# Attention beside a routed feed-forward layer on one core: heads normalised and stacked in pairs before the output projection, and another order of work where attention begins

## The chip, the core and the metric

The kernel runs on one core of a Trainium2 chip. The metric is the device time of one execution in microseconds (us). Five engines work side by side, each through its own list in order, and wait for each other by semaphores: TensorE (PE in the profile), VectorE (DVE), ScalarE (ACT), GpSimd (POOL) and SyncE (SP), which here only issues DMAs.

## The reference

Four sequences of 1024 tokens of 128 features are layer-normalised. The result goes through causal attention with 16 heads of 64 features, and through a mixture of 8 experts (two per token), whose sum is layer-normalised again. Both are added to the input.

```python
x = L0_attn_x
xn = _layernorm(x, axis=-1)
x = x + _L0_attn_ref(xn, ...) + _L0_ffn_ref(xn, ...)

# attention
normed = xn / l2 * dim ** 0.5 * gamma
q, k, v = split(normed @ w_qkv)          # 16 heads of 64
sim = einsum('bhid,bhjd->bhij', q * d ** (-0.5), k)
attn = softmax(where(causal_mask, mask_value, sim))
out = einsum('bhij,bhjd->bhid', attn, v)
return merge_heads(out) @ w_out          # 1024 -> 128
```

## The kernel before

The first block (up to about 284 us) normalises the tokens, chooses two experts for each, writes the tokens sorted by expert to DRAM, and runs the experts tile by tile; the results go back to DRAM by DMAs from ACT's queue. Then a barrier of all engines, and the second block: attention, and beside it the gathering and combining of the experts' results.

Attention goes over 8 pairs of heads (`hp`), in each over the 4 sequences, in each over the two heads of the pair: 64 rounds, which the text calls heads, 0 to 63. An even head and the odd one behind it are one pair on one sequence. A head's 1024 x 1024 score matrix, transposed (keys on partitions), is worked through in 12 chunks, c = 0 to 11: half 0 of the queries has chunks 0 to 3, half 1 chunks 4 to 11, each of 128 keys by 128 to 512 queries. `beside(g, c, last)` writes down what stands at chunk c of head g, and every engine walks the same list:

- `score` (lines 1302 to 1320): two matmuls, and a third one of the mask on the diagonal. ACT takes the exponential twice, once as float32 (`probs`), once rounded (`p_hi`), line 1082; POOL subtracts the two (`p_lo`, line 1033).
- `pv` (L1333, L1335, L1337), four chunks behind: three matmuls with the values; row 64 of the result, from a column of ones, is the softmax's denominator. After the last chunk of a half ACT copies the 65 x 512 result to `heads` (L1096).
- `max` (L1291, L1294 on PE, L1135 on DVE): the row maxima of the next head, in 8 parts, of which 4 to 7 are wide (640 to 1024 keys). They share one PSUM tile, so that PE's part m waits for DVE's part m-1 or m-2. `shift` turns the maxima by a transpose (L1300), ACT negates them, and SP lays them as a row of `q_b` by a DMA (L966); the first score of a half waits for it.
- `project` (L1261 to L1267): q, k and v of the next pair, with ACT's rounded copies (L1057, L1061), DVE's remainders (L1125, L1113), and four copies of 256 KB by SP (L954, L955).
- `y` and `add`, at chunks 6, 9 and 10: the output projection of the head before. A token tile is one matmul of 65 x 128 weights (the head's numerators and denominator) with the 65 x 129 matrix `wo`, whose corner passes the denominator on (L1350). DVE inverts it (L1191) and adds the scaled tile to `acc` (L1199).
- `combine` and `gather`: the experts' results, in heads 1 to 5 of each group of 8.

float32 matmuls count twice in the trace (two passes): `y` of a head has 8 matmuls, 16 passes, in groups of 6, 6 and 4.

The second block begins with splitting the first projection weights into a rounded part (ACT, L1048) and a remainder (DVE, L1105); then six projections, eight maxima and the first `shift` of head 0, and then the chunks.

## Time and profile before

| | |
|---|---|
| median of 3 runs | 1565.51 us (1565.09 to 1565.91) |
| the profiled execution | 1564.66 us |
| its span, first to last instruction | 1562.8 us |
| mean granted clock of TensorE | 0.969 |
| PE busy | 1449.6 us (93%) |
| DVE busy | 1076.4 us (69%) |
| ACT busy | 1067.4 us (68%) |
| POOL busy | 907.1 us (58%) |

A row of a timeline is: start in us, duration in us, engine, line and operation, output<-inputs with their forms, how many follow each other in it; in brackets the idle time before it and what ended that. PEld is the weight load of a matmul. Matmuls overlap, and a matmul's duration is longer than the distance to the next one: what a group of them costs PE is read from start to start.

### The profile page before, as it was taken

The numbers are of one execution on the slowest core, as the hardware profiler recorded it, in microseconds if no ns is written. First come the engines' busy times: TensorE is split into PE (matmuls) and PEld (weight loads), VectorE is DVE, ScalarE is ACT, GpSimd is POOL, SyncE is SP. The second block draws the span as 40 slices with busy tenths as digits, with TensorE's granted clock in tenths as the row PEclk, the third lists the DMA queues.
The fourth block names the chain that finished last, engine by engine and source line by source line (L and its number), as shares of the span: only waits on it lengthen the run. The fifth ranks groups of instructions, "written<-read, shape, count | busy, mean of one in ns | idle before, by whom it ended". The sixth has DMA issues, their size and how long they took to land.

```text
span 1562.8 us, 28739 instructions
## 1 busy us (share of the span) xinstructions
PE 1449.6 (93%) x9130; PEld 1126.8 (72%) x9131; DVE 1076.4 (69%) x2341; ACT 1067.4 (68%) x2590; POOL 907.1 (58%) x923
## 2 busy tenths in 40 slices
PE   3559999699999999999999999999999999999998
PEld 3548888467777777777777777777777777777776
DVE  6565555457776877687768776876687668866883
ACT  2445566267777777777777777777777777777775
POOL 0762000157666766676667666766676667666766
PEclk9579999689999999999999999999999999999999
DMA  9122211111111111111111111111111111111111
GB/s 311 46 79 71 58 54 52 44 35 42 33 28 38 40 33 29 38 40 33 29 38 40 33 28 40 38 33 28 39 38 33 28 41 37 33 28 42 37 28 55
DMA packets 58759, 72.34 MB, mean 46 GB/s; under 512 B 7400, under 2 KB 44560, under 8 KB 58640
## 3 DMA queue, kind: packets, MB, share of 16 engines
q1 hardware_dynamic: 40720, 52.57, 14.2%
q10 hardware_dynamic: 13824, 9.86, 2.0%
q0 software_dynamic: 4096, 8.40, 1.8%
q8 instruction: 65, 1.06, 0.3%
q14 instruction: 54, 0.44, 0.1%
HBM read 20.47 MB, written 16.52 MB: 24 GB/s over the span
## 4 chain that ended last, share of the span: by engine, by line
PE 66%; DVE 9%; ACT 3%; issue 2%; DMA 1%; SPq 0%; POOLq 0%; POOL 0%; DVEq 0%; ACTq 0%
PE max_ps L1291 9%; PE score_ps L1316 8%; PE score_ps L1317 8%; PE misc_ps L1350 8%; PE head_ps L1333 7%; PE head_ps L1337 7%; PE head_ps L1335 7%; PE misc_ps L1267 3%; DVE q_a L1125 3%; PE max_ps L1294 2%; PE score_ps L1319 2%; DVE row_max L1135 2%; ACT p_hi L1082 1%; PE misc_ps L1261 1%; PE misc_ps L1300 1%
## 5 line engine op out<-in xcount | busy, mean ns | idle before, releaser
L1033 POOL TENSOR_TENSOR p_lo<-probs,p_hi 128x512 fp32r<-128x512 f32 (+3 forms) x768 | 775.0, 1025 | 415.1 <-ACT p_hi L1082 408.7
L1082 ACT ACTIVATE probs<-score_ps 128x512 f32<-128x512 f32 (+3 forms) x768 | 375.4, 489 | 236.2 <-PE score_ps L1319 168.6
L1135 DVE TENSOR_REDUCE row_max<-max_ps 128x1 f32<-128x128 f32 (+7 forms) x512 | 386.7, 756 | 157.2 <-PE max_ps L1294 146.7
L1082 ACT ACTIVATE p_hi<-score_ps 128x512 fp32r<-128x512 f32 (+3 forms) x768 | 373.2, 486 | 0.0
L1333 PE MATMUL head_ps<-p_hi,v_hi 128*65 128x512 f32 (+3 forms) x768 | 295.2, 384 | 0.3 <-POOL p_lo L1033 0.3
L1316 PE MATMUL score_ps<-q_a,k_a 128*128 128x512 f32 (+3 forms) x768 | 266.6, 347 | 3.1 <-DMA q_b<-shift 3.1
L1317 PE MATMUL score_ps<-q_b,k_b 65*128 65x512 f32 (+3 forms) x768 | 266.9, 348 | 0.0
L1291 PE MATMUL max_ps<-k_a,q_a 128*128 128x384 f32 (+5 forms) x768 | 249.6, 380 | 16.4 <-DVE row_max L1135 12.6
L1337 PE MATMUL head_ps<-p_lo,v_hi 128*65 128x512 f32 (+3 forms) x768 | 258.7, 337 | 0.0
L1335 PE MATMUL head_ps<-p_hi,v_lo 128*64 128x512 f32 (+3 forms) x768 | 258.5, 337 | 0.0
L1316 PEld LDWEIGHTS score_ps<-q_a,k_a 128*128 128x128 f32 x768 | 144.8, 189 | 46.4 <-issue 3.7
L1291 PEld LDWEIGHTS max_ps<-k_a,q_a 128*128 128x128 f32 x768 | 144.6, 197 | 40.0 <-DVE row_max L1135 19.5
L1317 PEld LDWEIGHTS score_ps<-q_b,k_b 65*128 65x128 f32 x768 | 145.4, 189 | 16.7
L1350 PE MATMUL misc_ps<-wo,heads 65*128 65x129 f32 x1024 | 155.9, 285 | 1.3 <-ACT heads L1096 0.8
L1199 DVE SCALAR_TENSOR_TENSOR acc<-misc_ps,rden,acc 128x128 f32<-128x128 f32 x512 | 150.1, 345 | 6.8
L1337 PEld LDWEIGHTS head_ps<-p_lo,v_hi 128*65 128x65 f32 x768 | 104.0, 135 | 42.0
L1350 PEld LDWEIGHTS misc_ps<-wo,heads 65*128 65x128 f32 x1024 | 131.5, 194 | 2.0 <-issue 1.2
L1294 PE MATMUL max_ps<-ident,later 128*128 128x128 bf16 x512 | 118.8, 232 | 0.0
L1319 PE MATMUL score_ps<-later,ident 128*128 128x128 bf16 x512 | 118.7, 232 | 0.0
L1125 DVE TENSOR_TENSOR k_b<-misc_ps,k_a 64x512 fp32r<-64x512 f32 x128 | 88.1, 688 | 43.1 <-ACT k_a L1057 42.2
L1335 PEld LDWEIGHTS head_ps<-p_hi,v_lo 128*64 128x64 f32 x768 | 105.4, 137 | 15.2
L1333 PEld LDWEIGHTS head_ps<-p_hi,v_hi 128*65 128x65 f32 x768 | 108.7, 141 | 8.5 <-POOL p_lo L1033 0.8
(170 smaller groups left out, 2106.0 us busy)
## 6 DMA issues: line engine op xcount, KB each, us to landing
k_a<-k_a SPq DMA_DIRECT2D x64, 256.0 KB, 3.3
q_b<-q_a SPq DMA_DIRECT2D x64, 256.0 KB, 4.2
sorted_x<-zeros SPq DMA_DIRECT2D x13, 384.0 KB, 15.2
w_raw<-sorted_x SPq DMA_DIRECT2D x26, 192.0 KB, 2.5
sorted_y<-result ACTq DMA_DIRECT2D x78, 64.0 KB, 1.6
acc<-in_L_attn_x_dram SPq DMA_DIRECT2D x4, 512.0 KB, 9.0
w_raw<-in_L_ffn_W_dram ACTq DMA_DIRECT2D x1, 2048.0 KB, 22.7
q_b<-shift SPq DMA_DIRECT2D x128, 2.0 KB
```

What stands on the lines that cost most here:

```text
L1033: pool.tensor_tensor(p_lo[:, slot, 0:w], probs[:, slot, 0:w], p_hi[:, slot, 0:w].bitcast(F32), ALU.subtract).then_inc(p_split, 1)
L1082: ins = act.activation(p[:, (g * CH + c) % RING, 0:width], score_ps[(g * CH + c) % 2][:, 0:width], ACT.Exp, scale=SCALE)
L1135: dve.tensor_reduce(row_max[:, g % 2, t:t + 1], src, axes, ALU.max).then_inc(max_taken, 1)
L1199: ins = dve.scalar_tensor_tensor(out=row, in0=src[:, t, 0:D], scalar=rden[:, u % 2, t:t + 1], in1=row, op0=ALU.mult, op1=ALU.add)
L1291: ins = pe.matmul(max_ps[:, b, 0:w], rows, k_a[i][s][:, k0:k0 + w], start=True, stop=not last)
L1294: ins = pe.matmul(max_ps[:, b, w - P:w], later[:], ident16[:], start=False, stop=True)
L1316: pe.matmul(dst, k_a[i][s][:, keys], q_a[i][s][:, qs], start=True, stop=False)
L1317: ins = pe.matmul(dst, k_b[i][s][:, keys], q_b[i][s][:, qs], start=False, stop=not DIAG[c])
L1333: pe.matmul(head_ps[0:HEAD + 1, cols], v_hi[i][:, j, s], p_hi[:, slot, 0:width], start=(j == 0), stop=False)
L1335: pe.matmul(head_ps[0:HEAD, cols], v_lo[i][:, j, s], p_hi[:, slot, 0:width], start=False, stop=False)
L1337: pe.matmul(head_ps[0:HEAD + 1, cols], v_hi[i][:, j, s], p_lo[:, slot, 0:width], start=False, stop=c in LAST).then_inc(pv_done, 1)
L1350: ins = pe.matmul(dst[:, t * (D + 1):(t + 1) * (D + 1)], heads[:, g % 2, q0:q0 + P], wo[:, g % 2], start=True, stop=True)
```

## The change

1. **Stacked heads.** ACT's copy of a half (65 x 512) goes to `raw`. From there a chain of five steps runs in the list, at fixed numbers of chunks behind the last chunk of the half: SP folds the denominator row by a DMA to 16 x 32 (`fold`, 5), DVE inverts it (`invert`, 8), SP stores it to DRAM (`store`, 9), SP reads it back to 64 partitions (`spread`, 12), DVE multiplies the 64 x 512 numerators by it (`normalise`, 16) into `heads`, the even head of a pair in partitions 0 to 63, the odd one in 64 to 127. The output projection then has 128 rows and 128 columns without the denominator, once for the pair: four tiles (8 passes) at chunk 8 of the next even head, four at chunk 4 of the odd one behind it. DVE adds 128 x 512 in one instruction.
2. **Straight code.** The list is made once for all 64 heads; its counters are plain. `probs` has 4 buffers instead of 6, with a wait of ACT for POOL.
3. **Weights among the set-up work.** The split of the first projection weights stands in the first block. The wait for the experts' stored results goes from ACT's end of the first block to SP and POOL, ahead of the first gather.
4. **Wide maxima of the first head.** Only parts 0 to 3 stand ahead of its chunks; 4 and 5 stand at chunk 0, 6 at chunk 1, 7 at chunk 2. Head 1's maxima begin at chunk 3.

```diff
@@ set-up
+                    w_hi(act, 0)
                     act.wait_ge(set_up, 7)
                     act.sem_inc(waited, 1)
                     expert_steps(act, step)
-                    for n in range(RESULTS):
-                        act.wait_ge(expert_stored[n], 16 * (1 + len(range(n, SORTED, RESULTS))))
...
                         lower(u)
+                    w_lo(dve, 0)
...
@@ the list
+            CHAIN = [("fold", 5), ("invert", 8), ("store", 9), ("spread", 12), ("normalise", 16)]
+            FIRST_WIDE = {0: (4, 5), 1: (6,), 2: (7,)}
+            FIRST_MAX_AT = [3, 4, 5, 6, 7, 8, 9, 10]
-            Y_AT = [6, 9, 10]
-            y_units = [(0, 3), (3, 3), (6, 2)]
+            Y_AT = {8: 0, CH + 4: 1}
...
+                for kind, lag in CHAIN:
+                    if at >= lag and (at - lag) // CH < ALL_HEADS and (at - lag) % CH in LAST:
+                        order.append((kind, (at - lag) // CH, LAST.index((at - lag) % CH)))
...
@@ SP
+                    def fold_denominator(g, half):
+                        sp.wait_ge(raw_out, n_half(g, half) + 1)
+                        sp.dma_start(den[:, half], raw[HEAD:HEAD + 1, g % 2, half].rearrange("o (f n) -> o f n", f=FOLD)
+                                     ).then_inc(den_folded[half], 16)
+                    def store_inverse(g, half):
+                        sp.wait_ge(inverted, n_half(g, half) + 1)
+                        sp.dma_start(inv_rows[half].rearrange("(f n) -> f n", f=FOLD), inv[:, half]
+                                     ).then_inc(inv_stored[half], 16)
+                    def spread_inverse(g, half):
+                        sp.wait_ge(inv_stored[half], 16 * g + 16)
+                        sp.dma_start(scale[:, half], inv_rows[half].partition_broadcast(HEAD)
+                                     ).then_inc(scale_spread[half], 16)
...
@@ ACT
+                            if n_chunk(g, c) >= PROBS:
+                                act.wait_ge(p_split, n_chunk(g, c) - PROBS + 1)
...
+                            if g >= 2:
+                                act.wait_ge(normalised, n_half(g - 2, half) + 1)
+                            act.activation(raw[:, g % 2, half], head_ps[0:HEAD + 1, cols],
+                                           ACT.Copy).then_inc(raw_out, 1)
...
@@ DVE
+                    def invert(g, half):
+                        dve.wait_ge(den_folded[half], 16 * g + 16)
+                        dve.reciprocal(inv[:, half], den[:, half]).then_inc(inverted, 1)
+                    def normalise(g, half):
+                        cols = slice(half * BANK, (half + 1) * BANK)
+                        s = g % 2
+                        dve.wait_ge(scale_spread[half], 16 * g + 16)
+                        dve.tensor_tensor(heads[s * HEAD:(s + 1) * HEAD, cols], raw[0:HEAD, s, half], scale[:, half],
+                                          ALU.mult).then_inc(normalised, 1)
+                    def add_y(p, n, u):
...
+                        dve.wait_ge(misc_ready, u + 1)
+                        dve.tensor_tensor(acc[:, toks], misc_ps[u % 2][:].rearrange("p (t d) -> p t d", t=GROUP),
+                                          acc[:, toks], ALU.add).then_inc(y_added, 1)
...
@@ PE
+                    def project_out(p, n, u):
+                        dst = misc_bank(u)
+                        pe.wait_ge(normalised, n_half(2 * p + 1, n) + 1)
...
+                        for t in range(GROUP):
+                            q0 = (n * GROUP + t) * P
+                            ins = pe.matmul(dst[:, t * D:(t + 1) * D], heads[:, q0:q0 + P], wo[:],
+                                            start=True, stop=True)
+                        ins.then_inc(misc_ready, 1)
```

DVE in head 16 (an even one), chunks 5 to 10: `k_b` are the key remainders, `row_max` the maxima of head 17, `rden` and `acc` the inversion and addition of the output projection. Before:

```order
L1125 TENSOR_TENSOR k_b10<-misc_ps0,k_a10 64x512
L1125 TENSOR_TENSOR k_b11<-misc_ps0,k_a11 64x512
L1135 TENSOR_REDUCE row_max<-max_ps 128x1
L1191 RECIPROCAL rden<-misc_ps1 128x3
L1199 SCALAR_TENSOR_TENSOR acc<-misc_ps1,rden,acc 128x128 x3
L1135 TENSOR_REDUCE row_max<-max_ps 128x1
L1191 RECIPROCAL rden<-misc_ps1 128x3
L1199 SCALAR_TENSOR_TENSOR acc<-misc_ps1,rden,acc 128x128 x3
L1135 TENSOR_REDUCE row_max<-max_ps 128x1
```

The same place of the changed kernel:

```order
L1129 TENSOR_TENSOR k_b10<-misc_ps1,k_a10 64x512
L1129 TENSOR_TENSOR k_b11<-misc_ps1,k_a11 64x512
L1139 TENSOR_REDUCE row_max<-max_ps 128x1
L1193 RECIPROCAL inv<-den 16x32
L1199 TENSOR_TENSOR heads<-raw,scale 64x512
L1139 TENSOR_REDUCE row_max<-max_ps 128x1
L1206 TENSOR_TENSOR acc<-misc_ps1,acc 128x512
L1139 TENSOR_REDUCE row_max<-max_ps 128x1
```

Between the maxima of parts 5 and 6 the inversion and the multiplication of two earlier halves stand where the additions of the head before stood.

PE in head 16, chunks 6 to 9: `max_ps` are the maxima of head 17, `head_ps` the values, `misc_ps<-wo,heads` the output projection. Before:

```order
L1317 MATMUL score_ps0<-q_b00,k_b00 128x512
L1291 MATMUL max_ps<-k_a01,q_a01 128x448 x2
L1294 MATMUL max_ps<-ident16,later 128x128
L1350 MATMUL misc_ps1<-wo,heads 128x129 x3
L1333 MATMUL head_ps<-p_hi,v_hi0 65x384
...
L1291 MATMUL max_ps<-k_a01,q_a01 128x384 x2
L1294 MATMUL max_ps<-ident16,later 128x128
L1333 MATMUL head_ps<-p_hi,v_hi0 65x512
```

The same place of the changed kernel:

```order
L1316 MATMUL score_ps0<-q_b00,k_b00 128x512
L1290 MATMUL max_ps<-k_a01,q_a01 128x448 x2
L1293 MATMUL max_ps<-ident16,later 128x128
L1332 MATMUL head_ps<-p_hi,v_hi0 65x384
...
L1290 MATMUL max_ps<-k_a01,q_a01 128x384 x2
L1293 MATMUL max_ps<-ident16,later 128x128
L1346 MATMUL misc_ps1<-wo,heads 128x128 x4
L1332 MATMUL head_ps<-p_hi,v_hi0 65x512
```

The output projection leaves chunk 6 and stands at chunk 8, behind the part of the maxima that waits for DVE.

PE at the first head, from its fourth maximum on. Before:

```order
L1291 MATMUL max_ps<-k_a00,q_a00 128x512
L1294 MATMUL max_ps<-ident16,later 128x128
L1291 MATMUL max_ps<-k_a00,q_a00 128x512 x2
L1294 MATMUL max_ps<-ident16,later 128x128
...
L1291 MATMUL max_ps<-k_a00,q_a00 128x320 x2
L1294 MATMUL max_ps<-ident16,later 128x128
L1300 MATMUL misc_ps0<-ident,row_max 4x128
L1316 MATMUL score_ps0<-q_a00,k_a00 128x512
```

The same place of the changed kernel:

```order
L1290 MATMUL max_ps<-k_a00,q_a00 128x512
L1293 MATMUL max_ps<-ident16,later 128x128
L1299 MATMUL misc_ps0<-ident,row_max 4x128
L1315 MATMUL score_ps0<-q_a00,k_a00 128x512
L1316 MATMUL score_ps0<-q_b00,k_b00 128x512
L1318 MATMUL score_ps0<-later,ident16 128x128
L1290 MATMUL max_ps<-k_a00,q_a00 128x512 x2
L1293 MATMUL max_ps<-ident16,later 128x128
L1290 MATMUL max_ps<-k_a00,q_a00 128x448 x2
L1293 MATMUL max_ps<-ident16,later 128x128
```

The four wide maxima, ahead of the first score before, stand behind it.

## Rows read from the trace of the kernel before

**Rows 1.** Busy time by engine in a steady stretch: us, busy us (instructions) of each, clock, DMA

```profile
500.00:1000.00 500.00, 490.36 (x3098) 372.81 (x3098) 367.78 (x757) 371.33 (x855) 343.51 (x342) 1.00 0.16 36
```

**Rows 2.** Chain of waits, longest pieces: start us, us, what; once in eight heads

```profile
531.38 1.19 DVE gsc L1144
...
686.75 1.19 DVE gsc L1144
```

**Rows 3.** Timeline of head 16, an even one, chunks 6 to 9

```profile
639.49 0.89 PE L1350 MATMUL misc_ps<-wo,heads 65*128 65x129 f32 x6
...
640.13 0.42 PE L1333 MATMUL head_ps<-p_hi,v_hi 128*65 128x384 f32 x1
...
640.56 1.09 DVE L1135 TENSOR_REDUCE row_max<-max_ps 128x1 f32<-128x896 f32 x1
...
640.92 1.98 POOL L1033 TENSOR_TENSOR p_lo<-probs,p_hi 128x512 fp32r<-128x512 f32 x2 [1.20 <-ACT p_hi L1082]
...
641.98 0.52 PE L1291 MATMUL max_ps<-k_a,q_a 128*128 128x384 f32 x2
...
642.38 0.42 PE L1333 MATMUL head_ps<-p_hi,v_hi 128*65 128x512 f32 x1
```

**Rows 4.** Timeline of head 17, an odd one, chunks 3 to 5

```profile
652.49 1.84 POOL L1033 TENSOR_TENSOR p_lo<-probs,p_hi 128x384 fp32r<-128x384 f32 x2 [1.10 <-ACT p_hi L1082]
...
653.22 0.69 DVE L1135 TENSOR_REDUCE row_max<-max_ps 128x1 f32<-128x512 f32 x1 [0.82 <-PE max_ps L1294]
...
654.70 0.43 PE L1333 MATMUL head_ps<-p_hi,v_hi 128*65 128x512 f32 x1
...
655.66 1.11 PE L1267 MATMUL misc_ps<-w_raw,nT 128*128 128x128 f32 x8
...
656.53 0.30 PE L1333 MATMUL head_ps<-p_hi,v_hi 128*65 128x128 f32 x1
```

**Rows 5.** Groups by line and form: count, busy us, mean ns, idle before

```profile
L1181 DVE TENSOR_TENSOR x_row<-x_row,fbeta 128x512 f32<-128x512 f32 x8 | 5.4, 681 | 0.0
L1184 DVE TENSOR_TENSOR acc<-acc,x_row 128x512 f32<-128x512 f32 x8 | 13.4, 1669 | 0.3
L477 DVE RECIPROCAL tmp<-tmp 128x16 f32<-128x16 f32 x2 | 0.5, 253 | 0.1
L1350 PE MATMUL misc_ps<-wo,heads 65*128 65x129 f32 x1024 | 155.9, 285 | 1.3 <-ACT heads L1096 0.8 <-DVE acc L1199 0.5
```

**Rows 6.** Timeline of DVE in head 11, where the experts' results are combined

```profile
543.35 0.87 DVE L1199 SCALAR_TENSOR_TENSOR acc<-misc_ps,rden,acc 128x128 f32<-128x128 f32 x3
...
546.57 0.94 DVE L1135 TENSOR_REDUCE row_max<-max_ps 128x1 f32<-128x768 f32 x1
```

**Rows 7.** Timeline of the passage to attention

```profile
282.44 2.02 ACTq L425 DMA_DIRECT2D sorted_y<-result  x2
...
287.33 0.79 PE L1261 MATMUL misc_ps<-nT_hi,wqk_hi 128*128 128x512 f32 x1 [3.76 <-DVE wqk_lo L1105]
...
304.11 1.39 DVE L1135 TENSOR_REDUCE row_max<-max_ps 128x1 f32<-128x384 f32 x2 [0.32 <-PE max_ps L1294]
...
313.67 0.42 PE L1300 MATMUL misc_ps<-ident,row_max 128*4 128x128 f32 x1
...
314.42 9.38 SPq L966 DMA_DIRECT2D q_b<-shift  x2
...
316.28 0.76 PE L1316 MATMUL score_ps<-q_a,k_a 128*128 128x512 f32 x1 [2.19 <-DMA q_b<-shift]
```

**Rows 8.** Timeline of the last head's end

```profile
1554.66 0.59 ACT L1096 ACTIVATE heads<-head_ps 65x512 f32<-65x512 f32 x1 [2.37 <-PE head_ps L1337]
...
1558.52 0.61 DVE L1199 SCALAR_TENSOR_TENSOR acc<-misc_ps,rden,acc 128x128 f32<-128x128 f32 x2
```

**Rows 9.** DMA issues: what, queue, count, KB each, median us from issue to landing

```profile
sorted_y<-result ACTq DMA_DIRECT2D x78, 64.0 KB, 1.6
...
fgamma<-in_L_ffn_gamma_dram SPq DMA_DIRECT2D x1, 64.0 KB, 2.8
```

More of the change, by code:

```diff
@@ new lines, in attention_and_experts, with n_max, n_chunk, n_half @@
+            order += [("max", 0, m) for m in range(HALF_MAX[0] + 1)] + [("shift", 0, 0)]
+            for at in range(ALL_HEADS * CH + 2 * CH):
+                order += beside(at)
+            order = numbered(order)
+            misc_units = [o[:3] for o in order if o[0] in MISC_KINDS]
+            def n_max(g, m):
+                return g * PARTS + m
+            def n_chunk(g, c):
+                return g * CH + c
+            def n_half(g, half):
+                return g * 2 + half
+            def n_y(p, n):
+                return p * 2 + n
@@ new lines, in _ @@
+                    for kind, g, c, u in order:
+                        if kind == "score":
+                            score(g, c)
+                        elif kind == "max":
+                            max_scores_of(g, c)
+                        elif kind == "project":
+                            project(g, c, u)
+                        elif kind == "shift":
+                            shifts(g, c, u)
+                        elif kind == "pv":
+                            values(g, c)
+                        elif kind == "y":
+                            project_out(g, c, u)
```

448 lines of the change are left out of this document (188 added, 260 removed).

## The prediction, written before the changed kernel ran

> **What bounds the kernel now.** I read the busy times by window first. In a steady stretch of 500 us PE is busy 490.4 us at full clock, DVE 367.8, ACT 371.3 and POOL 343.5 [rows 1]. So the end is set by what stands in PE's list and by PE's few waits. The chain of waits shows a period: the same piece of the combination comes at 531.38 and at 686.75, so eight heads take 155.37 us [rows 2], 19.42 us a head. The reader should see that an engine with a quarter of its time free can still be late at one place, and PE has almost no free time in which that would be hidden. So I went from the shares to the timeline of an even and an odd head, at the places where the output projection leaves and arrives.
>
> **Passes of the output projection.** A group of 6 passes takes PE from 639.49 to 640.13, 0.64 us, or 0.107 a pass [rows 3]. A head has 16 passes, 1.71 us. Eight passes of 128 x 128 with 128 rows, which is what the new form has, take from 655.66 to 656.53, 0.87 us [rows 4]. The changed kernel has 8 passes a head on average, so a head loses 0.84 us of PE's list, 64 heads 53.8 us. The busy time of the group is 155.9 us for 1024 passes [rows 5], 0.152 a pass, but matmuls overlap there; the Trainium skill (Perfetto Trace Analysis, Identifying the Most-Contended Engine) says that matmul busy time is a bad measure because PE's instructions are pipelined. The spacing bears this out, and I take the spacing.
>
> **What PE now waits for, even head.** The projection left chunk 6 and stands at chunk 8, behind part 6 of the maxima. Before, it filled a hole: part 6 may start only when DVE has reduced part 5, at 640.56 + 1.09 = 641.65, and PE came there at 641.98 [rows 3]. DVE's reduction does not come earlier, since its input stands ahead of the projection in PE's list, and DVE went straight on to it from the key remainders. With the 0.64 us gone PE arrives at 641.34 and waits 0.31. Part 6 takes 0.40 (641.98 to 642.38), so PE is ready for the new projection at 642.05. That waits for `normalise`, which stands on DVE behind part 5 and the inversion. The inversion is 16 x 32; a 16-element reciprocal takes 0.253 [rows 5], twice that would be 0.51, and I take 0.38: until 642.03. The multiplication is not in the trace before. The nearest row is a float32 multiplication or addition of 128 x 512 with both inputs in SBUF: 0.681 us, but the like at another place takes 1.669 [rows 5]. What differs is whether POOL, which reads SBUF, is in an instruction. POOL is in two of them from 640.92 to 642.90 [rows 3]; by their widths (512 and 256) the first ends near 642.24. So the multiplication runs from 642.24 to 642.92, and the projection waits 0.87. Together 1.18 us of waiting in an even head, against 0.84 of passes saved: +0.34 us.
>
> The Trainium skill (SBUF — State Buffer, Who interferes with whom) says that a DVE instruction with two SBUF inputs contends with a GpSimd instruction that reads SBUF, and that the one issued second is fully blocked until the first is finished. The 1.669 beside the 0.681 agrees with it. The additions that go (L1199) have one input in PSUM, so this rule speaks against the change: the multiplications are 128 new instructions that can be blocked.
>
> **Odd head.** `normalise` stands behind part 3, which ends at 653.22 + 0.69 = 653.91; POOL is in two instructions from 652.49 to 654.33 [rows 4]. So it ends at 654.33 + 0.68 = 655.01. PE is at the projection's place at 654.70, where its next row starts now, and waits 0.31. With -0.84 this is -0.53 us.
>
> **Head 11 and its like**, one in eight, has DVE full of the combination. Part 6 is reduced at 546.57 [rows 6]. Ahead of it come new: two multiplications (1.36), the addition of 128 x 512 (0.68, by the same row), the inversion (0.38) and about 0.3 for the port; one addition of 0.87 goes [rows 6]. So part 6 is 1.85 later, and PE's part 7 with it. The four passes at chunk 10 (0.43) give some back: +1.4 us. In head 13, DVE's other full place, an inversion comes and a small addition goes; nothing.
>
> Eight heads: 4 x 0.34 - 3 x 0.53 + 1.4 = +1.2 us; eight times, +9.4. Heads 0 and 1 have no projection yet, which takes 0.3 + 1.2 = 1.5 off.
>
> **Edits that I cost at nothing.** ACT's wait for POOL with four buffers of `probs`: POOL is busy 343.5 of 500 us and PE itself needs the same result at the end of the chunk in which ACT needs it at the start. It would cost up to PE's whole loss of the wait, some 0.3 us a chunk, if POOL fell a chunk behind. The three DMAs of the chain: from SP's issue of the shift at 314.42 to the score that waited for it, 316.28, is 1.86 us [rows 7]; three times this and the inversion are 6 us, and the chain has 12 chunks of 1.6 us. Behind the chain's DMAs on SP stands the next shift, which needs to be there three chunks later; issue costs it well under a microsecond. If the fold lands late behind the four copies, DVE waits at the inversion in chunk 11, where its next maxima are not yet due. The two splits of the first weights go to the first block, behind its last work before the experts; there they lie beside the wait for the sorted tokens, and cost their own length at most, 0.8 us, if that wait is already over.
>
> **Passage.** PE's first projection started at 287.33, after ACT had issued the last store by 284.46 and waited for its landing (1.6, [rows 9]), the barrier, and the two splits [rows 7]. Without the landing and the splits it can start near 284.8: -2.5. At head 0 the fourth maximum is reduced by 304.11 + 1.39 = 305.50. From the transpose to the first score it took 313.67 to 316.28, 2.61 us [rows 7], so the first score comes near 308.1 instead of 316.3. But the four wide maxima are still one behind the other (305.5 to 313.7 before), and half 1 of the same head, at chunk 4, waits for them and for another 2.6 us. They now start at 309 and share PE with scores and projections, which is about 319.5 + 2.6 = 322. Head 1's parts 1 to 3 still follow. I take -1.5 of the 8.2. Bounds: 0 and -6.
>
> **End.** ACT's last copy ends at 1555.25, DVE's last addition at 1559.13, the span at 1562.8: 3.9 us and 3.7 for the output [rows 8]. Now: fold 1.9, inversion 0.4, store 1.6 (nearest row [rows 9]), spread 2.8 (a broadcast from DRAM, [rows 9]), multiplication 0.7, eight passes 0.9 at full and 1.8 at half clock, which I take since PE has been idle, addition 0.7, and 0.3 for hand-overs: 10.2 us against 3.9. +6.3 us, bounds +4 and +9. [...]
>
> **Sum.** 9.4 - 1.5 - 2.5 - 1.5 + 6.3 = +10.2. The profiled execution took 1564.66 us, so 1574.9; the median of the runs is 0.85 above it: 1576 us. So the saved passes are paid back by waits, and the longer end remains.
>
> **Rivals.** First, **no port waits**: DVE's multiplication never meets POOL. Then the even head waits 0.31 + 0.66, +0.13; the odd one 0, -0.84; head 11's like +1.1. Eight heads -0.9, 64 heads -7.2: 1564.66 - 7.2 - 1.5 - 4.0 + 6.3 + 0.85 = 1559 us. For it: POOL is idle a third of the time. Against: in both walks it is in an instruction just then. Second, **the waits do not show, PE stays the bound**: -53.8 - 4.0 + 6.3 gives 1514 us. It needs DVE to reach part 5 over 1 us sooner; against it stands that its inputs (ACT's copies of the projection at chunk 5) have not moved. These two are not slower than before; the turn is where an even and an odd head together wait less than 1.7 us, minus head 11's share. Third, **POOL takes the port first**: when its first instruction ends POOL's second goes before the multiplication. Then the even head waits until 642.90 instead of 642.24, 0.66 more, 31 times, and head 11's like 0.7: +26 us, 1602 us. Against: the 1.669 is less than a whole POOL instruction of 1.3 on top of 0.68. Fourth, **the reordered first head gives nothing**, since the chain of the wide maxima sets chunk 4: 1577.5 us, inside the first case's range.
>
> **How the numbers follow.** The forecast, with the fourth rival in it: 0.60 (own range 1564 to 1592). No port waits: 0.16. PE the bound, or waits between that and the last: 0.09. POOL first, or a late fold: 0.15. The range for 8 in 10 is 1546 to 1600; it leaves out the full gain and the far end of the third. About 0.2%, 3.1 us, is what a measurement can tell from no change. Faster (below 1562.4): most of rivals one and two, 0.23. Same: the low edge of the forecast and a part of rival one, 0.15. Slower: 0.62.
>
> **What the profile would show.** Spacing of `misc_ps<-wo,heads` 0.11 us a pass, 512 passes. In even heads, waits of PE at part 6 for `row_max` (0.3) and at the projection for `heads` (0.9), in odd ones 0.3 at the projection. `heads<-raw,scale` with a mean near 1 us, above 0.68. Eight heads 155 to 158 us. The passage 4 us shorter, the end 6 longer. Eight heads below 152 us would make the forecast wrong, and a mean of 0.7 for the multiplication would show that the port did it; waits for the DMA `scale` or `den` would show a chain that I took as hidden.

## The result, and the profile after

The changed kernel takes **1661.4 us** (1659.3 to 1661.8, 4 runs) against 1565.3 us (1563.7 to 1565.9, 4 runs) of the kernel before, run beside it: a ratio of 1.061 (95%: 1.060 to 1.063). It is slower, as forecast, but by 96 us and not by 11; the range ended at 1600. The profiled execution has a span of 1659.6 us.

The row of the page after that answers to the clock, and the shares of its chain of waits:

```profile
PEclk9579999799999999999999999999999999999998
...
PE 46%; DVE 23%; POOL 5%; issue 4%; ACT 4%; DMA 1%; SPq 0%; POOLq 0%
```

DVE holds 23% of the chain now; on the page before it was 9%, and PE's share 66%. The busy times of the stretch of [rows 1], in the same columns, after:

```profile
500.00:1000.00 500.00, 458.64 (x2680) 334.17 (x2678) 361.38 (x562) 341.57 (x794) 320.06 (x311) 0.96 0.19 46
```

PE is 41 us idle where it was 10, and its clock isn't full any more. No engine is busier than before in this stretch. Over the whole execution DVE is 51 us busier (1127.3 against 1076.4), POOL 21 and PE 6, for a span that is 97 us longer. So the time went into PE's waits and, as its clock says, into slower work. I measured each head from the first score matmul of one to that of the next, in the eight heads r0 to r7 (heads 16 to 23) that make one period:

```text
                              r0     r1     r2     r3     r4     r5     r6     r7    sum
before                      19.84  18.33  19.84  19.81  19.83  18.32  21.10  18.29  155.4
after                       20.09  17.65  20.90  25.47  21.52  23.27  20.65  17.63  167.2
before, no combination      19.84  18.33  19.84  18.31  19.83  18.32  19.86  18.31  152.6
after, no combination       20.08  17.65  20.86  17.65  20.07  17.65  20.50  17.66  152.1
```

(The lower two are e2 and e1 below.) An ordinary even head is 0.25 us longer (r0), an ordinary odd one 0.68 shorter (r1). The loss stands in r2 to r5, 13.4 us a period. In r3, r4 and r5 DVE also combines the experts' results, in 21 steps that the text calls parts 0 to 20; r2 has none of them, and its 1.06 is there without the combination too.

**The ordinary heads.** The timeline after at the places of [rows 3] and [rows 4]:

```profile
660.42 3.66 POOL L1053 TENSOR_TENSOR p_lo<-probs,p_hi 128x512 fp32r<-128x512 f32 x3 [1.22 <-ACT p_hi L1091]
661.07 0.33 DVE L1193 RECIPROCAL inv<-den 16x32 f32<-16x32 f32 x1
...
661.43 0.82 DVE L1199 TENSOR_TENSOR heads<-raw,scale 64x512 f32<-64x512 f32 x1
...
662.39 1.13 PE L1346 MATMUL misc_ps<-wo,heads 128*128 128x128 f32 x8 [0.50 <-DVE heads L1199]
...
672.25 1.83 POOL L1053 TENSOR_TENSOR p_lo<-probs,p_hi 128x384 fp32r<-128x384 f32 x2 [1.11 <-ACT p_hi L1091]
...
673.69 0.94 DVE L1199 TENSOR_TENSOR heads<-raw,scale 64x512 f32<-64x512 f32 x1
```

The chain of inversion, multiplication and projection is as forecast; the multiplication lasts 0.82 beside POOL where 0.68 is its length when it meets nothing. PE shows no idle time at part 6, where 0.31 was walked, and 0.50 at the projection.

**Head r3.** Before, the three copies at the start of the head, and PE's only long wait in it, at part 4:

```profile
686.75 1.19 DVE L1144 COPY gsc<-mean 128x4 f32<-128x4 f32 x1
687.85 0.16 DVE L1145 COPY gsc<-rstd 128x4 f32<-128x4 f32 x1
687.92 1.25 DVE L1146 COPY gsc<-weights 128x8 f32<-128x8 f32 x1
...
693.51 0.73 PE L1291 MATMUL max_ps<-k_a,q_a 128*128 128x512 f32 x2 [0.99 <-DVE row_max L1135]
```

POOL, DVE and PE after, at the start of the head and ahead of its part 6:

```profile
703.56 7.09 POOL L1053 TENSOR_TENSOR p_lo<-probs,p_hi 128x256 fp32r<-128x256 f32 x7
...
706.87 3.39 DVE L1148 COPY gsc<-mean 128x4 f32<-128x4 f32 x1
710.17 0.15 DVE L1149 COPY gsc<-rstd 128x4 f32<-128x4 f32 x1
...
714.13 1.69 DVE L1199 TENSOR_TENSOR heads<-raw,scale 64x512 f32<-64x512 f32 x1
714.15 0.73 PE L1290 MATMUL max_ps<-k_a,q_a 128*128 128x512 f32 x2 [1.36 <-DVE row_max L1139]
...
715.96 1.30 PE L1346 MATMUL misc_ps<-wo,heads 128*128 128x128 f32 x5 [1.00 <-DVE heads L1199]
...
721.24 0.69 DVE L1117 TENSOR_TENSOR v_lo<-misc_ps,v_hi 128x512 fp32r<-128x512 f32 x1 [2.52 <-ACT v_hi L1073]
...
722.85 2.34 DVE L1163 SCALAR_TENSOR_TENSOR x_row<-two_y,gsc,x_row 128x128 f32<-128x128 f32 x4
725.11 0.34 DVE L1193 RECIPROCAL inv<-den 16x32 f32<-16x32 f32 x1
725.37 1.49 DVE L1199 TENSOR_TENSOR heads<-raw,scale 64x512 f32<-64x512 f32 x1
...
727.58 0.93 DVE L1139 TENSOR_REDUCE row_max<-max_ps 128x1 f32<-128x768 f32 x1
...
728.56 0.56 PE L1290 MATMUL max_ps<-k_a,q_a 128*128 128x320 f32 x2 [2.71 <-DVE row_max L1139]
```

A copy of 4 elements a partition takes 3.39 us (1.19 before, [rows 2]) while POOL runs seven instructions one behind the other; the next copy of the same size takes 0.15. The three copies together take 3.8 us where they took 2.4. What stands next in DVE's list is late: PE waits 1.36 at part 4 (0.99 before) and 1.00 at the projection, whose multiplication lasts 1.69.

The second cluster is another matter. At 721.24 DVE itself had been idle for 2.52 us, so the copy's lateness is no longer in its list. PE's wait of 2.71 at part 7 comes from what stands on DVE between parts 5 and 6: four SCALAR_TENSOR_TENSOR, an inversion, a multiplication of 1.49 and four statistics, 4.73 us where it was 3.43 (before from 698.51 to 701.94, after from 722.85 to 727.58). e5, which has no copies, has the same wait.

**Head r5**, an odd head too:

```profile
767.69 3.45 POOL L1053 TENSOR_TENSOR p_lo<-probs,p_hi 128x512 fp32r<-128x512 f32 x3 [0.47 <-ACT p_hi L1091]
...
766.73 1.03 DVE L1199 TENSOR_TENSOR heads<-raw,scale 64x512 f32<-64x512 f32 x1
767.69 3.78 DVE L1179 TENSOR_SCALAR x_row<-x_row,gmom,gvar 128x128 f32<-128x128 f32 x4
771.40 0.94 DVE L1139 TENSOR_REDUCE row_max<-max_ps 128x1 f32<-128x768 f32 x1
...
772.39 0.90 PE L1290 MATMUL max_ps<-k_a,q_a 128*128 128x320 f32 x2 [3.79 <-DVE row_max L1139]
```

Four TENSOR_SCALAR of 0.33 us take 3.78, beside three instructions of POOL; PE waits 3.79 us.

**The clock.** Windows after; columns as in [rows 1]:

```profile
716.00:719.40 3.40, 3.40 (x14) 2.90 (x15) 2.72 (x6) 0.00 (x0) 0.00 (x0) 0.51 0.02 5
...
730.00:733.40 3.40, 3.40 (x13) 2.44 (x13) 0.88 (x8) 2.05 (x4) 1.27 (x1) 0.54 0.01 1
771.00:778.00 7.00, 5.61 (x19) 4.00 (x20) 4.88 (x10) 1.86 (x4) 1.37 (x2) 0.53 0.05 12
```

Behind the waits in r3 and from the middle of the one in r5 PE runs at the lower of its two levels (1.2 GHz), though it has work. The stretches at half clock between 330 and 1500 us add up to 92 us; before there are none. If all of that were work, it would have cost 46 us, which is an upper bound. PE's busy time points the same way: 1455.6 us for 8618 instructions, against 1412.1 for as many in e1 below, which has no such stretch.

**Passage and end.** After, in the order of [rows 7] and [rows 8]:

```profile
286.02 0.77 PE L1260 MATMUL misc_ps<-nT_hi,wqk_hi 128*128 128x512 f32 x1 [1.35 <-PEq L285]
...
302.08 1.39 DVE L1139 TENSOR_REDUCE row_max<-max_ps 128x1 f32<-128x384 f32 x2 [0.32 <-PE max_ps L1293]
...
306.18 0.77 PE L1315 MATMUL score_ps<-q_a,k_a 128*128 128x512 f32 x1 [2.19 <-DMA q_b<-shift]
...
1645.55 0.59 ACT L1107 ACTIVATE raw<-head_ps 65x512 f32<-65x512 f32 x1 [2.67 <-PE head_ps L1336]
...
1647.88 0.34 DVE L1193 RECIPROCAL inv<-den 16x32 f32<-16x32 f32 x1 [2.77 <-DMA den<-raw]
...
1652.37 0.68 DVE L1199 TENSOR_TENSOR heads<-raw,scale 64x512 f32<-64x512 f32 x1 [0.52 <-DMA scale<-inv_rows]
...
1653.20 2.04 PE L1346 MATMUL misc_ps<-wo,heads 128*128 128x128 f32 x8 [2.08 <-DVE heads L1199]
1655.28 0.69 DVE L1206 TENSOR_TENSOR acc<-misc_ps,acc 128x512 f32<-128x512 f32 x1 [2.23 <-PE misc_ps L1346]
```

The fourth maximum is 2.0 us earlier and the first score 10.1, but head 1 starts at 336.17 against 336.25: nothing of it is left. From ACT's last copy (1646.14) to DVE's last addition (1655.97) it is 9.8 us; 10.2 were forecast, 3.9 it was.

### The profile page after: what moved, and what is told of

Its sections match the earlier page's. It is cut to its first block, busy times and chain, and to the rows that moved or that the text cites. A ratio compares the mean times of both kernels' runs of the same rounds, so it can differ in the third digit from the quotient of the medians.

```text
span 1659.6 us, 27795 instructions
## 1 busy us (share of the span) xinstructions
PE 1455.6 (88%) x8618; PEld 1095.1 (66%) x8619; DVE 1127.3 (68%) x1957; ACT 1059.9 (64%) x2590; POOL 927.7 (56%) x921
## 4 chain that ended last, share of the span: by engine, by line
PE 46%; DVE 23%; POOL 5%; issue 4%; ACT 4%; DMA 1%; SPq 0%; POOLq 0%
PE max_ps L1290 6%; DVE row_max L1139 5%; PE head_ps L1332 5%; PE head_ps L1336 5%; PE score_ps L1316 5%; PE head_ps L1334 5%; PE score_ps L1315 5%; PE misc_ps L1346 5%; DVE heads L1199 4%; PE misc_ps L1266 3%; POOL p_lo L1053 3%; DVE k_b L1129 3%; DVE q_a L1129 2%; DVE x_row L1179 2%; POOL two_y L1046 2%
## 5 line engine op out<-in xcount | busy, mean ns | idle before, releaser
L1053 POOL TENSOR_TENSOR p_lo<-probs,p_hi 128x512 fp32r<-128x512 f32 (+3 forms) x768 | 794.3, 1050 | 485.5 <-ACT p_hi L1091 479.5
L1290 PE MATMUL max_ps<-k_a,q_a 128*128 128x384 f32 (+5 forms) x768 | 259.6, 393 | 73.4 <-DVE row_max L1139 66.4
L1315 PE MATMUL score_ps<-q_a,k_a 128*128 128x512 f32 (+3 forms) x768 | 276.4, 360 | 3.1 <-DMA q_b<-shift 3.0
L1316 PE MATMUL score_ps<-q_b,k_b 65*128 65x512 f32 (+3 forms) x768 | 275.5, 359 | 0.0
L1336 PE MATMUL head_ps<-p_lo,v_hi 128*65 128x512 f32 (+3 forms) x768 | 265.2, 345 | 0.0
L1334 PE MATMUL head_ps<-p_hi,v_lo 128*64 128x512 f32 (+3 forms) x768 | 264.8, 345 | 0.0
L1316 PEld LDWEIGHTS score_ps<-q_b,k_b 65*128 65x128 f32 x768 | 150.9, 196 | 17.6
L1199 DVE TENSOR_TENSOR heads<-raw,scale 64x512 f32<-64x512 f32 x128 | 120.8, 944 | 7.5 <-DMA scale<-inv_rows 5.5
L1129 DVE TENSOR_TENSOR q_a<-misc_ps,q_a 64x512 fp32r<-64x512 f32 x128 | 88.2, 689 | 42.5 <-ACT q_a L1069 40.3
L1346 PE MATMUL misc_ps<-wo,heads 128*128 128x128 f32 x512 | 79.6, 304 | 39.4 <-DVE heads L1199 31.5
```

The costliest lines, as they stand in the source:

```text
L1053: pool.tensor_tensor(p_lo[:, slot, 0:w], probs[:, n_chunk(g, c) % PROBS, 0:w], p_hi[:, slot, 0:w].bitcast(F32), ALU.subtract).then_inc(p_s ...
L1129: ins = dve.tensor_tensor(lo, src[s * HEAD:(s + 1) * HEAD, :], hi, ALU.subtract)
L1199: dve.tensor_tensor(heads[s * HEAD:(s + 1) * HEAD, cols], raw[0:HEAD, s, half], scale[:, half], ALU.mult).then_inc(normalised, 1)
L1290: ins = pe.matmul(max_ps[:, b, 0:w], rows, k_a[i][s][:, k0:k0 + w], start=True, stop=not last)
L1315: pe.matmul(dst, k_a[i][s][:, keys], q_a[i][s][:, qs], start=True, stop=False)
L1316: ins = pe.matmul(dst, k_b[i][s][:, keys], q_b[i][s][:, qs], start=False, stop=not DIAG[c])
```

## The experiments

Each was timed beside the kernel before (medians of 1564.5 to 1565.3 us); gains and losses are against the medians above. Sums are those of r0 to r7.

**e1 and e2: no combination.** Parts 0 to 20 only count their semaphores, in the changed kernel and in the kernel before.

> The changed kernel with the arithmetic that combines the experts' results on DVE left out (its waits, gathers and counters stay). In its trace heads 16 to 24 take 167.2 us: four heads without combination take 17.6 to 20.7, and heads 19 and 21, where DVE combines, 25.5 and 23.3 against 19.8 and 18.3 before. Theory A (the loss stands where the combination meets the new DVE work; PE waits there for the maxima and its clock falls behind the wait): eight heads fall to 4 x 20.1 + 4 x 17.65 = 151 us, the kernel to 1661 - 8 x 16.2 = 1532 us, no half clock in the steady part. Rival B (the loss is in all heads, from the chain of DMAs or the port): it stays near 1640. Rival C (the passage and the end hold it): near 1640 too, with eight heads at 151.

> The kernel before with the same arithmetic left out: the measure for the run beside it. Heads 16 to 24 take 155.4 us, with one head of 21.1 and one odd of 19.8 that the combination lengthens. Without it 4 x 19.84 + 4 x 18.3 = 152.6 us: 1565 - 22 = 1543 us. Theory A: the changed kernel without combination is then faster than this by 1.6 us in eight heads, about 13 us less 2 to 6 for its longer end: within 5 to 15 us below. Rival B: it is slower than this by 80 us or more.

1542.1 us (1541.2 to 1543.1) and 1543.9 us (1543.3 to 1545.3). Without the combination the two kernels differ by 1.9 us. So the combination costs 21.4 us before and 119.3 us after: the difference, 98 us, is the whole loss. It is the combination beside the new work that costs; neither of them does it alone.

**e3: the normalising instruction reads one tile in SBUF.**

```diff
-                        dve.tensor_tensor(heads[s * HEAD:(s + 1) * HEAD, cols], raw[0:HEAD, s, half], scale[:, half],
-                                          ALU.mult).then_inc(normalised, 1)
+                        dve.tensor_reduce(heads[s * HEAD:(s + 1) * HEAD, cols], raw[0:HEAD, s, half].unsqueeze(2),
+                                          AX_X, ALU.max).then_inc(normalised, 1)
```

> The changed kernel with the multiplication of 64 x 512 replaced by a reduction over one element, which reads raw alone: the normalisation is left out, the instruction, its place, its waits and the 64 x 512 output stay. It tells the share of the two SBUF inputs (0.94 us mean against 0.615 at least). Rival D (the port): the loss of 96 us falls by half or more. Theory A: each of 16 multiplications in eight heads is 0.3 us shorter; where PE waits for it that is 4 x 0.3 in even heads and little in odd ones, and in heads 19 and 21 0.5 to 1 us each: 3 us in eight heads, 1661 - 24 = 1637 us, the big waits in heads 19 and 21 still there.

1600.8 us (1597.7 to 1602.0), sum 160.4: 61 of the 96 us are gone. So having two SBUF inputs in 128 instructions is most of it, though not by their own length alone (the excess over 0.68 is 0.26 us, 34 us in all, much of it off PE's path). Two more things move with the edit. POOL is shorter too: its 768 subtractions take 765.7 us in place of 794.3, those of 128 x 256 0.74 in place of 0.90, so each side waits for the other. And the ordinary heads gain as well (r1 is at 17.38). The long copy stays: 2.89 us. The operation changes with the input, from a multiplication to a reduction, so the 61 us are the edit's and not a clean price of the input.

**e4: the combination at other places**, with nothing left out.

```diff
-            COMBINE_AT = [(g, c) for g in (3, 4, 5) for c in (0, 2, 3, 6, 7, 10, 11)][:10 + RSQRT_STEPS]
+            COMBINE_AT = ([(2, 9), (3, 4), (4, 9), (5, 4), (5, 9), (6, 0)] + [(6, 9)] * 8
+                          + [(7, 0)] * 2 + [(7, 1)] * 2 + [(7, 4), (7, 9), (7, 11)])
```

> The changed kernel, complete, with the 21 steps of the combination at other places of the list: the long ones at chunk 9 of even heads and chunk 4 of odd ones of each eight (heads 2 to 7), where DVE has a hole behind its maxima, the short ones together at chunk 9 of head 6 and chunks 0 and 1 of head 7. Theory A: the waits of 2.7 and 3.8 us and the half clock behind them go; eight heads come to 151 to 154 us and the kernel to 1661 - 8 x 14.5 = 1545 us, below the kernel before. Rival B, C or D: it stays above 1620, since the amount of DVE work is the same.

1610.0 us (1607.4 to 1610.5). 51 us gone, r4 and r5 back to 20.1 and 17.65, but r3 at 25.54. POOL and DVE there:

```profile
689.42 0.97 POOL L1048 DMA_INDIRECT two_y<-sorted_y,places  x1 [0.16 <-issue]
690.40 7.84 POOL L1055 TENSOR_TENSOR p_lo<-probs,p_hi 128x512 fp32r<-128x512 f32 x7
...
690.83 0.95 DVE L1150 COPY gsc<-mean 128x4 f32<-128x4 f32 x1
691.69 6.58 DVE L1151 COPY gsc<-rstd 128x4 f32<-128x4 f32 x1
698.19 0.16 DVE L1152 COPY gsc<-weights 128x8 f32<-128x8 f32 x1
```

The second copy lasts 6.58 us, through six of POOL's seven instructions, and ends at 698.27, when the last of them ends (698.24). From this I formed **theory E**: a copy of DVE from SBUF to SBUF can go on waiting while POOL's instructions follow each other without a pause, not for one of them only.

**e5 and e6: no copies**, on the changed kernel and on e4. The code is straight, so the parts can read the tiles themselves.

```diff
-                            dve.tensor_copy(gsc[:, 0], mean[:, toks])
-                            dve.tensor_copy(gsc[:, 1], rstd[:, toks])
-                            dve.tensor_copy(gsc[:, 2:4], weights[:, :, toks]).then_inc(comb_step, 1)
+                            dve.sem_inc(comb_step, 1)
...
-                                ins = dve.tensor_scalar(x_row[:, q], x_row[:, q], gsc[:, 0, q:q + 1],
-                                                        gsc[:, 1, q:q + 1], ALU.subtract, ALU.mult)
+                                ins = dve.tensor_scalar(x_row[:, q], x_row[:, q], mean[:, t0 + q:t0 + q + 1],
+                                                        rstd[:, t0 + q:t0 + q + 1], ALU.subtract, ALU.mult)
```

> The changed kernel with its combination at its own places, but without the three tiny copies of part 0 (gsc<-mean, rstd, weights, L1148 to L1150): the code is straight now, so the parts read mean, rstd and weights themselves. Nothing of the result is left out. Theory E (DVE's copies from SBUF to SBUF find their port held by POOL and go on waiting through several of POOL's instructions that stand back to back, until POOL pauses): in the changed kernel the copy gsc<-mean waits 3.39 us at 706.87, head r3 of eight lasts 25.47 us. Without the copies r3 loses 3.4 us and some of its time at half clock, comes to 20.5 to 22 us, r5 stays near 23; 8 x 3.5 to 8 x 4.5 less, 1625 to 1634 us. Rival F (it is only the amount and place of DVE's work): the copies themselves cost 0.16 us each without a wait, 0.5 us per eight heads, 1656 to 1660. Rival G (the wait only passes to the next instruction, the TENSOR_SCALAR of part 1): r3 stays within 1 us of 25.47, 1653 to 1661.

> The kernel of the moved combination (1610.0 us) without the three tiny copies of part 0. There the copy gsc<-rstd lasted 6.59 us in each of eight rounds while POOL ran six p_lo instructions back to back, and ended 0.03 us after POOL's first pause; head r3 lasted 25.54 us. Theory E: r3 comes to 19 to 20 us, the eight heads from 160.4 to 154 to 155, half clock in the steady part nearly gone, 1558 to 1566 us. Rival F (amount and place of DVE's work): 0.5 us per eight heads, 1604 to 1607. Rival G (the wait passes to the next instruction of DVE that needs the port): r3 stays above 23 us, above 1590.

e5: 1634.6 us (1632.3 to 1636.3), 27 less, r3 at 22.55. DVE's multiplication and PE's wait at part 7 of r3 in e5:

```profile
713.25 1.50 DVE L1198 TENSOR_TENSOR heads<-raw,scale 64x512 f32<-64x512 f32 x1
...
716.44 0.56 PE L1289 MATMUL max_ps<-k_a,q_a 128*128 128x320 f32 x2 [2.74 <-DVE row_max L1139]
```

Without the copies the first cluster of r3 is as it was before (0.98 at part 4, no wait at the projection, full clock); the second is untouched.

e6: **1545.0 us** (1543.0 to 1547.7), 65 less than e4, every odd head at 17.65 and no stretch at half clock; a ratio of 0.988 (0.986 to 0.990) to the kernel before. At e4's places three copies whose bare length is under 0.5 us cost 65 us. e6 came out better than theory E's 1558 to 1566. The copy's 6.4 us above its bare length are 51 us; the expectation left out that e4 also has 47.8 us at half clock, which bounds the rest by 24.

**e7: no gathers** in the changed kernel (POOL's eight indirect DMAs a period).

> The changed kernel with the eight indirect DMAs of each eight heads left out (POOL doesn't issue them; the combination adds x_row in place of the gathered rows, so that arithmetic is not the reference's). Each of them occupies POOL 0.97 us between its p_lo instructions. Theory E with the gathers as the cause of POOL's being behind: POOL has 7.8 us less in r1 and r2, is no longer back to back at 706.87, the copy gsc<-mean takes under 1.3 us, r3 comes to 21 to 22.5 us; r5, three heads after the last gather, stays near 23: 1625 to 1637 us. Rival (POOL is back to back without the gathers too, from its own 1.25 us waits beside DVE): the copy still waits over 2.5 us, 1650 to 1660.

1626.7 us (1625.8 to 1627.7), r3 21.68, r5 22.84. The groups of the multiplications, of part 18 and of the first copy, which takes 1183 ns in place of 3392:

```profile
L1197 DVE TENSOR_TENSOR heads<-raw,scale 64x512 f32<-64x512 f32 x128 | 110.3, 861 | 7.9 <-DMA scale<-inv_rows 5.9
...
L1177 DVE TENSOR_SCALAR x_row<-x_row,gmom,gvar 128x128 f32<-128x128 f32 x32 | 33.5, 1101 | 0.0
...
L1146 DVE COPY gsc<-mean 128x4 f32<-128x4 f32 x8 | 9.5, 1183 | 0.0
```

POOL's backlog in r3 comes from the gathers, as theory E has it; r5's loss does not, nor does PE's wait at part 7 of r3 (2.74 here). r2 is back at 20.02: its loss is the gathers'.

**e8: all maxima of head 0 ahead of its chunks**, undoing the last edit alone.

> The changed kernel with the first head as in the kernel before: all eight maximum parts of head 0 ahead of its first chunk, nothing beside its chunks. It undoes the last of the change's three edits alone. In the changed kernel the first chunk starts 10.1 us earlier (306.18 against 316.28) but head 1 starts at 336.17 against 336.25. Theory that the reordering gains nothing, since the wide maxima beside the chunks hold them up (chunk 0 to 4 in 14.19 us against 8.67): within 0.8 us of the changed kernel's 1661.4, both signs. Prediction's own step: 1.5 us more, 1662.9. Rival (the wide maxima cost more than they give): 1.5 us or more less.

1660.2 us (1655.4 to 1661.0). Head 1 starts at 332.85 in place of 336.17, but e11 against e6, the same edit, has it at 334.99 in place of 333.66. The medians differ by 1.2 and 1.1 us, within their spread: what the reordered first head gives or costs is too small to be told here.

**e9: the combination of the kernel before at e4's places.**

> The kernel before with its combination at the places of e4 and e6, its three tiny copies kept (its rounds are a loop whose number isn't known when the code is built, so the parts need them). Nothing left out. It asks what stacking adds to the 1545.0 us of e6. Theory E: with the parts where POOL is not behind, the kernel before gets back nearly all that its combination costs (1564.5 against 1543.9 without it), unless a copy at (2, 9) starts beside a back-to-back stretch of POOL: 1545 to 1552 us without such a wait, 1575 to 1610 with one of 3 to 6 us in each eight heads. Rival F (amount of DVE's work, not the place): 1560 to 1568.

1555.7 us (1555.5 to 1559.4), 0.995 (0.993 to 0.996) of before, sum 153.9. It lies outside all the expected ranges, 4 us above the nearest: the moving helps there too, by 10 of 21 us, and e6 is 11 us below it.

**e10: the copies as two-input instructions**, in e4.

One of the three:

```diff
...
-                            dve.tensor_copy(gsc[:, 1], rstd[:, toks])
...
+                            dve.tensor_tensor(gsc[:, 1], rstd[:, toks], rstd[:, toks], ALU.max)
...
```

> The kernel of e4 (moved combination, 1610.0 us) with its three tiny copies of part 0 at their place, each written as a TENSOR_TENSOR (the maximum of a tile with itself, two inputs in SBUF) in place of a COPY. Nothing left out. It tells the form of the instruction from its place. If the form decides (a COPY goes on waiting while POOL's instructions follow one another without a pause, a TENSOR_TENSOR gets its turn after one of them, as heads<-raw,scale did with at most 1.75 us): no instruction of part 0 lasts over 1.4 us, r3 comes to 18 to 19 us, 1546 to 1556 us. If the place decides (any instruction of DVE on SBUF alone would wait there): one lasts over 5 us, r3 over 24 us, 1600 to 1612.

1605.1 us (1600.1 to 1606.8). Groups of DVE between 400 and 1500 us:

```profile
L1151 DVE TENSOR_TENSOR gsc<-rstd 128x4 f32<-128x4 f32 x7 | 46.1, 6591 | 0.0
```

The place decides and not the form: the same 6.59 us. The part of theory E that gave this to copies alone is refuted.

**e11 and e12: toward a faster kernel.** e11 is e6 with the maxima ahead; e12 is e11 with `Y_AT = {9: 0, CH + 5: 1}`.

> The kernel of e6 (1545.0 us) with all eight maximum parts of head 0 ahead of its first chunk, as in the kernel before. Nothing left out. In e8 that edit by itself moved the start of head 1 from 336.17 to 332.85 us, and the median from 1661.4 to 1660.2. If the reordering of the first head costs: 1 to 3.5 us less than e6, 1541.5 to 1544. If it gains what the prediction gave it (1.5 us): 1546.5. If neither: within 0.8 of 1545.0.

> The kernel of e11 with the output projection of a pair one chunk later (its halves at chunk 9 and at chunk 5 of the next head, before 8 and 4), so that the DMA of the scale and the normalising multiplication have a chunk more. Nothing left out. In e6 an even head waits 0.7 us for heads L1199 at L1345 in its chunk 4 or 8 and lasts 20.05 to 20.9 us. Theory (that wait is what an even head loses): 0.3 to 0.7 us less for each of some 32 pairs, 8 to 20 us less than e11. Rival (PE is the bound in an even head, 11 chunks and 16 maximum parts and passes one after the other, and the wait's time comes back elsewhere): within 2 us of e11.

e11 1543.9 us (1542.9 to 1546.4), not to be told from e6. e12 **1524.7 us** (1520.7 to 1526.4), a ratio of 0.974 (0.972 to 0.975): it beats both kernels. The waits of PE for the multiplication, in e11 and then in e12:

```profile
PE misc_ps L1347 <- DVE heads L1200: 19.0, 36, 3.6
```

```profile
PE misc_ps L1347 <- DVE heads L1200: 5.6, 2, 3.6
```

(us in total, times, longest.) 13 us less waited there, and 19 gained.

**e13: r5's parts at other chunks of r5**, in the changed kernel: chunks 0, 0, 1, 1, 4, 9, 11 in place of 0, 2, 3, 6, 7, 10, 11.

> The changed kernel with the seven last parts of the combination in the same head r5, at its chunks 0, 0, 1, 1, 4, 9, 11 in place of 0, 2, 3, 6, 7, 10, 11 (the chunks at which they stand in e6, there in r7). Nothing left out, nothing else changed. In the changed kernel the four TENSOR_SCALAR of part 18 at chunk 7 wait beside POOL for 1.0 to 1.35 us each and the maximum part behind them is 3.8 us late; r5 lasts 23.27 us. Theory E (the place beside the normalising multiplication, the projections' subtractions and POOL decides, not the amount of work): r5 comes to 17.7 to 19 us, 8 x 4.3 to 8 x 5.6 less: 1617 to 1627 us. Rival F (amount of DVE's work in the odd head, which is one period of 17.65 us of PE's work): r5 stays above 21.5 us, above 1647.

1629.6 us (1624.0 to 1631.9); r5 at 17.65, r6 at 23.40 in place of 20.65. DVE in r5:

```profile
757.64 1.10 DVE L1181 TENSOR_SCALAR x_row<-x_row,gmom,gvar 128x128 f32<-128x128 f32 x4
```

The same four TENSOR_SCALAR take 1.10 in place of 3.78, and the whole loss of r5 is gone with the same amount of work. The 2.75 in r6 I had not expected: part 20 at chunk 11 takes 3.2 us of DVE (two instructions of 128 x 512) just ahead of the key and query remainders of r6, and PE waits 2.04 for them. (In the mean of seven periods r6 is 1.8 longer.)

**e14 to e16: the projection later**, in the changed kernel (`{9: 0, CH + 5: 1}`), the kernel before (`Y_AT = [8, 9, 10]`), and once more in e12 (`{10: 0, CH + 6: 1}`).

> The changed kernel with the output projection of a pair one chunk later (chunk 9, and chunk 5 of the next head, before 8 and 4), nothing else. From e12 (19 us less than e11 in 32 pairs, 0.6 us each): 15 to 25 us less, 1636 to 1646, if the chunk's gain is that of PE's wait for heads<-raw,scale (31.5 us of waits at L1346 in the changed kernel). Rival (the pieces add: the multiplication's lateness in r3 to r5 comes from DVE's being behind there, and is as late at the next chunk): within 5 us of 1661.

> The kernel before with its output projection at chunks 8, 9, 10 in place of 6, 9, 10. Nothing left out. It has no reciprocal spread by a DMA and no multiplication ahead of the projection. If the later projection helps only where that chain stands ahead of it: within 4 us of 1565, either sign. If it helps in itself (PE's order in a head): 8 us less or more.

> The kernel of e12 (1524.7 us) with the projection one more chunk later (chunk 10, and chunk 6 of the next head). Nothing left out. In e12 no wait of PE at the projection over 0.1 us is left between 800 and 960 us, so that theory gives nothing more: within 3 us of 1524.7. Rival (the places of the projection among PE's other work are worth something by themselves): 4 us less or more.

1633.8 us (1631.8 to 1637.0), 1604.7 us (1604.0 to 1605.3) and 1539.6 us (1537.4 to 1540.4). In e14 the waits at the projection fell from 31.5 us to 5.9, 27.6 us were gained, even heads are 0.5 us or more shorter, but r3 and r5 are at 26.67 and 22.95: what remains there is DVE's lateness at the maxima. e15 fell outside both expectations: 39.7 us slower, all heads 0.1 to 0.7 longer and r6 at 22.86. e16 is 15 us above e12, mostly in r2 (22.13 against 20.40). In both the new waits are for DVE: in r6 of e15 PE waits 2.05 for the query remainders (0.98 before), in r2 of e16 1.46 and 1.19 for maxima, where e12 has no such wait. So the projection's chunk also counts by what stands on DVE beside it; no run separates that further.

## Why the prediction was wrong

- **Ordinary heads: right in r0, r1, r4 and r7.** Without the combination (e1 against e2) r0 and r4 are 0.24 longer for +0.34 forecast, the odd heads 0.66 shorter for 0.53. In r0 the projection waited 0.50 for the multiplication where 0.87 was walked, in r1 0.12 where 0.31 was. But r2 and r6 are 1.02 and 0.64 longer even then, so the period changes by -0.5 us and not by the -0.76 of four even and four odd heads. In the medians e1 is 1.9 us below e2; the sum with head 11 as an ordinary odd head is -5.2 us.
- **Passage: wrong in sum, by 4 us.** Forecast were 2.5 for the barrier and the splits and 1.5 for the reordered first head; head 1 starts 0.1 us earlier. The first part was right: from the end of the last store's issue to the first projection it is 0.47 us where it was 2.88 (285.55 to 286.02, 284.45 to 287.33), though the first block ended 1.1 later in this profile. The reordered first head gave nothing that can be told from its spread (e8, e11), so the fourth rival was nearer. Head 1, which has no projection beside it any more, is 1.8 shorter (16.67 against 18.49) where 1.7 was counted.
- **End: right.** +5.4 us by the length of the last head to the end, +6.3 forecast; the fold took 1.7, store and spread 1.4 and 2.8.
- **The failed steps are "Head 11 and its like ... +1.4 us" and "In head 13, DVE's other full place, an inversion comes and a small addition goes; nothing".** They measured +5.66 (r3) and +4.95 (r5), and the even heads beside them, which had only the +0.34 of every even head, +1.69 (r4) and +1.06 (r2; its excess is the gathers', e7).
  - In r3 the wait that the prediction walked is there, at part 7, but 2.71 us long for 1.85, and PE then runs at half clock for 3.4 us. With the copies out (e5) r3 is 2.7 us above before for 1.4 forecast. The new instructions had been counted by bare length and "about 0.3 for the port"; the multiplication ahead of part 6 lasts 1.49, and the four instructions ahead of it 2.34 where they took 1.62.
  - The rest of r3, 2.9 us a period or 27 us in the median (e5), is the copy, which was counted at nothing new. Each wait for POOL was taken as one instruction long at most. The Trainium skill (SBUF — State Buffer, Who interferes with whom), which the prediction followed, says that the one issued second is blocked until the first is finished. The multiplications bear that out (mean 0.94, longest 1.75), but the copies do not: 3.39 and 6.58 us, through three and six of POOL's instructions.
  - Head 13 was passed over because the number of its instructions hardly changed, while what counts is that four SBUF instructions meet POOL just ahead of a maximum part (3.78 us for 1.10 in e13); e13 shows it, with the same work at other chunks.
- **A reading that was off:** the 0.681 and the 1.669 of [rows 5] were told apart by whether POOL is in an instruction. In the trace POOL is in one at both; beside the 0.681 it is POOL's that is long (1.85 us for 128 x 512, 1.29 otherwise). The price falls on either engine, and the sum had it on DVE alone.
- **The step that was missing** is PE's clock. The prediction took half clock at the end alone. A wait of 2.7 us costs more than 2.7 when what follows runs at half; that is bounded above by 46 us of the 96. PE's busy time is 43.5 us above e1's for as many instructions, and most of that should be the clock, but no run isolates it (in e4 it is 27.9 above e6's, where the clock can give 24 at most).
- **Rivals.** "POOL takes the port first" (1602, chance 0.15) had what the copies do, but gave it to the multiplications of the ordinary even heads, where it did not happen, and 0.7 us to head 11's like. No wait for `den` or `scale` in the steady part mattered (12.8 and 5.5 us of DVE's idle time in the whole run): the DMA chain was hidden, as forecast. That POOL would be behind was cost at "some 0.3 us a chunk" for ACT; the price came at DVE instead.

What stays open: why one SBUF instruction of DVE gets its turn after a single instruction of POOL (part 18 in r5: 1.35, 1.03 and 1.29 us for 0.33) and another waits through six. In both long waits POOL had just fallen behind, and without the gathers the wait was a single instruction's (e7, 1.18); e10 excludes the form. But the 3.39 us copy ended at 710.26, at the end of POOL's last instruction but one (710.23), while POOL's stretch went on to 710.65, so "until POOL pauses" is not the whole rule either, and no run looked for it. The losses measured by e3, e5, e7, e13 and e14 overlap and do not add up to a split of the 96 us.

## What to carry to other kernels

A new instruction is to be priced at the fullest stretch of its engine's list and not at an average one: there it makes the next wide result late, PE waits, and its clock can fall with the wait. Before adding SBUF-to-SBUF work on DVE, look in the timeline for stretches in which POOL runs without a pause, and put small DVE copies anywhere else, or read the source directly: three copies of under 0.5 us were worth 65 us in e4 and 27 in the changed kernel. When a change moves one consumer, move the other work of that engine with it: the change costs 96 us with the combination's old places and, with the combination moved, the direct reads and a later projection (e12), gains some 40; the kernel before gains 10 by the moving alone (e9).

## What the runs showed of the hardware that was not expected

- A DVE instruction of 4 elements a partition lasted 6.58 us beside back-to-back GpSimd instructions, through six of them (e4), and the same with one input (COPY) as with two (TENSOR_TENSOR, e10): 6.59 mean over 8 and 8 instances. It ended 0.03 us after the last of them.
- GpSimd waits as well: its subtractions of 128 x 256 take 0.90 us on average in the changed kernel and 0.74 in e3, where DVE's instruction beside them reads one tile.
- TensorE fell to its lower level (granted 0.51 to 0.54) for 3.4 us after waits of 1.4 us with 1 us of another close by and of 2.7 us, and for 6.8 us around one of 3.8 us, in a stretch in which it was otherwise over 90% busy; e6 and e12 have no such stretch.
